# A mixture-of-experts pipeline in which ScalarE applies the gate of a tile one iteration later

## The reference

```python
x = x + jnp.tanh(g_xattn[0]) * xattn(layernorm(x), ctx, ctx)
# the experts, on xf = layernorm(x), 4096 rows:
logits = xf @ Wr + br
topv, _ = lax.top_k(logits, 2)
weights = softmax(where(logits >= topv[:, 1:2], logits, -inf))
h = gelu(einsum('td,edh->eth', xf, W1) + b1[:, None, :])      # 256 -> 1024
expert_out = einsum('eth,ehd->etd', h, W2) + b2[:, None, :]   # 1024 -> 256
x = x + jnp.tanh(g_ffn[0]) * einsum('etd,te->td', expert_out, weights)
```

## Time and profile before

| | us |
|---|---|
| median of three runs | 892.22 |
| the profiled execution, its own time | 895.73 |
| its span, first to last instruction | 893.9 |
| TensorE matmul busy | 786.2 |
| VectorE busy | 582.6 |
| ScalarE busy | 486.0 |
| GpSimd busy | 352.4 |

### The profile page before, as it was taken

How to read it: one execution, slowest core, us unless ns; L and a number is a source line. 1 busy time by engine, 2 the same in 40 slices (tenths; PEclk the granted TensorE clock), 3 DMA queues, 4 the chain that set the end, 5 groups by cost and what they waited for, 6 DMA issues and landing times. The chain is left out here.

```text
span 893.9 us, 27595 instructions
## 1 busy us (share of the span) xinstructions
PE 786.2 (88%) x8684; PEld 720.4 (81%) x8685; DVE 582.6 (65%) x1457; ACT 486.0 (54%) x1205; POOL 352.4 (39%) x390
## 2 busy tenths in 40 slices
PE   4499999999999999998539879999999999999993
PEld 3389888898888889898439778888888888888882
DVE  2368999999999988988735345554555555555442
ACT  2156656665555556665225445666555555556652
POOL 2234655555555565546411122222222222222222
PEclk9699999999999999999659999999999999999996
DMA  8875888777778899974366975333334333332212
GB/s 183 147 140 128 162 179 173 137 148 155 162 167 211 196 220 191 191 156 151 132 149 155 271 113 70 52 51 47 49 50 51 47 49 50 51 51 26 25 21 28
DMA packets 124028, 105.84 MB, mean 118 GB/s; under 512 B 60928, under 2 KB 117632, under 8 KB 121728
## 3 DMA queue, kind: packets, MB, share of 16 engines
q1 hardware_dynamic: 110032, 85.51, 46.4%
q0 software_dynamic: 13296, 18.23, 13.0%
q10 hardware_dynamic: 576, 0.56, 0.2%
HBM read 36.54 MB, written 32.19 MB: 77 GB/s over the span
## 5 line engine op out<-in xcount | busy, mean ns | idle before, releaser
L1265 POOL DMA_INDIRECT out_rows<-yg,gates x71 | 114.6, 1614 | 321.1 <-ACT yg L1299 288.0
L1426 PE MATMUL bank<-wts,hh 128*128 x1704 | 203.9, 276 | 24.8 <-DVE hh L1321 21.5
L1290 ACT ACTIVATE hf<-bank,b1t,gscale 128x128 f32<-128x128 f32 x568 | 206.4, 468 | 31.5 <-issue 17.6
L1412 PE MATMUL bank<-xh,wts 128*128 128x128 f16 x3408 | 204.4, 220 | 15.2 <-issue 15.2
L1412 PEld LDWEIGHTS bank<-xh,wts 128*128 x3408 | 198.8, 99 | 16.8 <-issue 15.2
L1426 PEld LDWEIGHTS bank<-wts,hh 128*128 128x128 f16 x1704 | 162.7, 99 | 57.3 <-issue 37.2
L1320 DVE TENSOR_SCALAR hh<-hf,hscale 128x512 f16<-128x512 f32 x142 | 69.1, 486 | 201.6 <-ACT hf L1290 199.9
L1044 PE MATMUL bank<-va,probs 128*128 128x102 f32 x1024 | 139.7, 278 | 9.0 <-DVE ao L740 9.0
L540 POOL TENSOR_SCALAR_AFFINE_SELECT xh<-rowmax 128x512 bf16<-128x512 bf16 x128 | 94.2, 736 | 135.7 <-DVE rowmax L792 127.5
L1044 PEld LDWEIGHTS bank<-va,probs 128*128 128x128 f32 x1024 | 126.3, 193 | 12.2 <-DVE ao L740 6.8
L1299 ACT ACTIVATE yg<-yb,gates 128x256 f32<-128x256 f32 x71 | 36.1, 508 | 157.3 <-DVE yb L1331 140.7
(11 more groups left out here) (169 smaller groups left out, 975.6 us busy)
## 6 DMA issues: line engine op xcount, KB each, us to landing
wts<-in_W SPq DMA_DIRECT2D x16, 1024.0 KB, 7.1
wts<-keys SPq DMA_DIRECT2D x96, 128.0 KB
wts<-queries SPq DMA_DIRECT2D x96, 128.0 KB, 5.5
split_weights<-wts SPq DMA_DIRECT2D x8, 1024.0 KB, 5.1
wts<-split_weights SPq DMA_DIRECT2D x8, 1024.0 KB, 7.4
xin<-in_x SPq DMA_DIRECT2D x16, 256.0 KB, 2.7
cin<-in_ctx_in SPq DMA_DIRECT2D x16, 256.0 KB, 3.1
out_rows<-x SPq DMA_DIRECT2D x16, 256.0 KB, 4.4
```

Of the source, the lines that this page charges most:

```text
L1265: pool.indirect_dma_start(out=out[:, :], out_offset=bass.IndirectOffsetOnAxis(ap=numbers, axis=0), in_=yg[m % 2][:, :], in_offset=None, co ...
L1290: last = act.activation(hf[b][:, c, :], HB[2 * b + half][:, c % 4 * TILE:(c % 4 + 1) * TILE], ACT.Gelu, bias=b1t[:, bass.ds(e, 1), c], sca ...
L1412: last = pe.matmul(HB[2 * b + half][:, c % 4 * TILE:(c % 4 + 1) * TILE], weight(expert[1], first_at(wp, k, c), P), xh[(m + 1) % RING][:, x ...
L1426: last = pe.matmul(YB[b][:, 0:D], hh[b][:, hp, c, :], weight(expert[0], second_at(wp, c), D), start=q == 0, stop=q == 23)
```

## The change

ScalarE takes the gate of tile i-1 in iteration i, where it took that of tile i. The wait for yb is shifted with it. The wait for the scatter-add is still for the tile two before the one gated, so in iteration i it is for i-3. All engines' pipelines get one more iteration at the end, in which ScalarE gates the last tile and the others have nothing to do but count a semaphore.

```diff
-            peeled(first + RING * rounds, hi)
+            peeled(first + RING * rounds, hi + 1)
...
-                    if there(0):
-
-                        e = expert_of(act, i)
-                        act.wait_ge(yb_ready, i + 1)
-                        when(act, before(i, 2), added, added_value(i - 2))
-                        act.activation(yg[m % 2][:, :], yb[m % 2][:, :], ACT.Copy,
-                                       scale=gates[m][:, bass.ds(e, 1)]).then_inc(yg_ready, 1)
+                    if there(-1):
+
+                        e, p = expert_of(act, i - 1), (m - 1) % 2
+                        act.wait_ge(yb_ready, i)
+                        when(act, before(i, 3), added, added_value(i - 3))
+                        act.activation(yg[p][:, :], yb[p][:, :], ACT.Copy,
+                                       scale=gates[(m - 1) % RING][:, bass.ds(e, 1)]).then_inc(yg_ready, 1)
```

## The result

The changed kernel takes 862.91 us, the median of four runs from 856.86 to 865.78; the kernel before took 891.93 beside it. The profiled execution took 861.33 us, its span is 859.6. Here and in the experiments, executions that were disturbed or lie over 1.5% above the fastest of their kernel (870.33 and 1327.64 us of the changed kernel, 896.94 and 1580.65 us of the kernel before) stay out of the ratios.

A forecast was written before the change was run, and what follows sets the result against it. A loop through ScalarE and VectorE, 5.68 us per tile, was taken to pace TensorE. Steady stage -18.3, start -6.6, tail +2.25 gave -22.6 us, from 892.22 to 869.6; range 866 to 880 (own range 866 to 876).

The forecast's parts named there:

- The bound: Expert stage: a loop of gelu, split, yb and gate through ScalarE and VectorE, 5.68 us per tile, paces TensorE.
- TensorE's own pace: Expert stage: 5.30 us per tile plus 0.12 for register loads in every fourth y product, 5.42 in all.
- about 5.8 once: Middle of the expert stage, sign of being right: TensorE periods of 5.30 three times and about 5.8 once.
- The count of periods: Steady stage, y(10) to y(70): 60 periods, each falling from 5.725 to 5.42, a gain of 18.3 us.
- The tail: End of the kernel, counted from y(70): 18.4 us instead of 16.15, a cost of 2.25; bounds 0 and 4.7.
- The start: First expert tiles, to y(10): one tile more slack on slow scatter-adds gains 6.6 us; bounds 0 and 8.
- The end: Last three scatter-adds: 6.0, 10.7 and 15.3 us after h(70) starts, a chain of 4.66 each; span ends at 23.7.
- A: Steady stage: TensorE's own stalls, hidden by the loop's waits, make its period 5.55 to 5.6; gain 9, time 879; 8%.
- B: Start: gives nothing, as the scatter-add chain begins 3.3 us later and keeps that lag; time 876; 12%.
- C: Steady stage: TensorE already at its own pace of 5.73, so cutting the loop gains nothing; slower, 894.5 to 898; 4%.
- the sum's own bound of 25.5 for a flat 5.30: Steady stage: upper bound of the gain, 25.5 us, with TensorE at 5.30 for every tile.

The follow-up runs named there:

- The fill of 0.37 us: One more VectorE instruction, a fill of a 128x256 scratch tile, ahead of each yb: added to the kernel before 914.56 us, to the changed kernel 863.02 us.

## Why the prediction was too small

**The bound: right.** TensorE's high busy share hid a loop of 5.68 us through ScalarE and VectorE. The fill of 0.37 us lengthened the tile by 0.37 before and by nothing after.

**TensorE's own pace: the step that failed.** The prediction took the gap of 0.48 at y(2) for every fourth y product and so 5.42 per tile. The rows it read the earlier trace rows are at tiles 2 to 4. The gap belongs to the bounds check, which the program makes only for tiles below 16; with the check kept everywhere the pace is 5.412, almost the forecast 5.42, and without it 5.307 to 5.317. The difference of 0.10 to 0.11 over 59 periods is 6 us. The listed code has it, `skip_runtime_bounds_check_because=... if i >= RING`, and the prediction doesn't take it into account. Its sign of being right, "about 5.8 once" in four periods, didn't come either: all periods from y(11) to y(69) are 5.30.

**The count of periods: an error of 2.8 us.** The sum had 60 periods from y(10) to y(70). In the changed kernel y(70) comes straight behind y(69), since there is no h(71): 837.78 and 5.40 us for both. Only 59 are whole periods, and the last is 2.62 instead of 5.42. The tail, counted from y(69) as in the table, was thus forecast at 2.62 + 18.4 = 21.0 and measured at 21.82; against the 21.93 of before it costs nothing, where the sum charged 2.25. With both put right the forecast is 59 x (5.725 - 5.307) = 24.7, 6.6 at the start and 21.93 - 21.0 = 0.9 at the end, together 32.2 and a time of 860.0, against 29.9 of the two profiles: these have 0.6 less in the steady part, 0.9 less at the start and 0.8 less at the end.

**The start: right in kind, within the bounds, its size a matter of the execution.** Forecast -6.6, measured -5.75, -1.92 and -6.37 in three executions of the changed kernel, each against the one profile of the kernel before (with the fill on VectorE its start took 63.80 where this one took 64.56). The forecast followed the landings through: scatter 0 later (8.42 us behind y(0) instead of 5.28), stalls before y(8) and y(9), which are there (2.10 and 2.58, forecast 1.6 and 1.8 to 3.9). The clock dropped in one of the three. What the rows of before did not give is how much the distance of the scatter-adds varies while the weights stream in: 9.16 to 9.92 there, 7.2 to 10.9 in the three executions.

**The end: its chain right, its cost too high by the miscount above.** Scatter-adds 68 to 70 were forecast 6.0, 10.7 and 15.3 us after h(70) starts (837.78 - 2.68 = 835.10); they came at 6.6, 11.6 and 15.9. The y products of the end run at full speed.

**The rivals.** A (stalls of TensorE's own) went the other way: there are fewer than were seen. B (the start gives nothing) came near in one execution of three. C is out: TensorE does a tile in 5.30. The pace of 81 ns per matmul in a stream of weight loads and matmuls, which the prediction quotes from the Trainium skill ("TensorE: Matmul & The Clock Gate", section "Back-to-back issue gap"), is not borne out in this kernel: 48 in 2.68 us are 55.8 ns, tile after tile, with TensorE busy 100.00 of 100 us.

**The range** ended at 866 because TensorE's own period was taken as known at 5.42; the sum's own bound of 25.5 for a flat 5.30 was written down and left out of it. The limit of 0.2% for what can be told was too fine as well: executions of the kernel before, in the comparisons, lie between 883.58 and 896.45.

## What to carry to other kernels

An engine that is 95% busy can still be paced by a loop through others. It shows as many short waits of the busy engine on the same releaser, and a period that equals the sum of a chain that leaves the busy engine out; a small extra instruction in the chain proves it. When an engine's own pace is read from a few undisturbed tiles, read the program for what is special about these tiles, and count the periods of a pipeline's end by hand. Where a buffer comes free late only while something else loads, more buffers help: two more of 128x256 f32 gave here 6.5 us (863.51 and 857.0, the gate in the same place, on one chip).

## Not expected of the hardware

- The attention stage, the same code in all these kernels, ended at times 8.9 us apart: y(0) between 464.90 and 473.78 over twelve profiled executions. It can be a large part of the spread of the times.
- A bounds check of one loaded group of expert numbers on TensorE costs 0.39 to 0.66 us of its time even where nothing else holds TensorE, and once 1.03 (3.01 and 3.04 us from y to the next h, 3.10 in the earlier trace rows, instead of 2.62).
- While weights stream in, a scatter-add of 128 rows of 256 values follows the one before after 7.2 to 10.9 us in the three executions of the changed kernel, against 4.38 and 4.96 at its end. With one of them 2 us later the start took 62.64 us instead of 58.19; 1.5 us of that are the y product at the lower clock (4.32 instead of 2.78).
